# Graph layer chain on one core: in the pruning loop, the load of a later block is issued ahead of the store of the pruned block

## The chip, the cores and the metric

The kernel runs on 1 core of one Trainium2 chip. The metric is the device time of one execution in microseconds (us). A core has five engines that run their own instruction streams and meet at semaphores: TensorE (PE), VectorE (DVE), ScalarE (ACT), GpSimd (POOL) and SyncE (SP), which here issues nearly all transfers (DMAs). The page counts 16 DMA engines for them.

## The reference, cut to what matters

x is 4096 x 64, adj is a 4096 x 4096 matrix of float32 (64 MB) with about 0.2% of its entries nonzero. Four graph layers follow one another, each with a residual and a layer norm. The third (L2) runs two iterations of an attention and pruning layer with H = adj; of an iteration, this is what the change touches:

```python
# x_comp: x times the mask of nodes that stay; xn: its rows normed
cos = xn @ xn.T
edge_scores = jax.nn.softmax(cos * H / TAU, axis=1)
edge_mask = (edge_scores >= th_edge) & comp_mask[:, None]
H_pruned = H * edge_mask
connectivity = H_pruned.sum(axis=1)
...
edeg = jnp.maximum(H_pruned.sum(axis=0), EPS)
...
agg = H_pruned.T * dv_isqrt[None, :] @ transformed
msg = dv_isqrt[:, None] * (H_pruned @ agg * de_inv[:, None])
```

(The last two lines are joined here.) So each row block of H is read, scored, pruned and written to memory, and the whole of H_pruned is read again afterwards.

## The kernel before, in words

The matrix doesn't fit on the core, so each pass streams it in 32 row blocks of 128 x 4096 float32, 2 MB (2048 KB) each. The passes run in phases, one after the other, with a barrier of all engines between phases. The two iterations (`for it in range(2)`) each have an attend phase, which scores all blocks against edge features, and a prune phase. In the prune phase, after a short part that makes the mask of nodes, comes the pruning loop over n = 0 to 31, written out without a hardware loop. The block of step n is `seq[n]`.

The buffers of the loop: `held`, 5 slots (HELD = 5) for blocks of H as read, block n in slot n % 5; and `prod`, 3 slots (SL3 = 3), block n in slot n % 3, for its scores, which are turned in place into exponentials and then into the pruned block. Blocks 0 to 3 are still there from the attend phase; `load(R)` with R = 4 loads block 4 at the start.

The work of block n on the engines:

- TensorE (`score_products`, L848) makes the scores in four chunks of 1024 columns in PSUM; later (`column_sum`, L866) it adds up the columns of the pruned block. That waits for `pruned`.
- DVE (`weighted_scores`, L884) multiplies each of the four chunks with the block of H into `prod` and takes the row maximum (L889).
- ScalarE (`exponentials`, L895) takes exp in place with the row sum.
- DVE (`prune`, L1205 and L1210) compares with the threshold, multiplies with H, and writes the pruned block into `prod`, counting up `pruned`.
- SP (L1080) stores the pruned block to `Hp` ("pruned" in the profile), counting `stored`.

DVE's order is: scores of block n + 1, pruning of block n, scores of block n + 2, pruning of block n + 1, and so on. Before the scores of block n it waits for three things: that block n is loaded (`loaded[n % 5]`), that the store of block n - 3, from the same `prod` slot, has landed (`stored[n % 3]`), and that the column sums of block n - 3 are done (`summed`).

SP runs one queue of instructions in order. In step n it waits until block n is pruned, then issues two DMAs: the store of block n (L1080), and the load of block n + 5 (L1075) into the `held` slot that the pruning of block n has just set free. Steps 27 to 31 have no load. In steps 28 and 29 SP also issues the first two loads of chunks of `Hp` (`load_chunk`, L1066) for what follows, after waiting for stores of much earlier steps; the third comes once all scores are made, the rest after all stores landed. All these DMAs go to the same queue.

After the loop, the gather and scatter part reads `Hp` in 32 chunks and is mostly TensorE work.

Of the kernel before, what the change touches and what calls it, by code (L numbers as in the profile page):

```python
# [88 lines left out]
def build(nc, d):  # L89
    ctx = ExitStack()  # L90
    with ctx:
# [57 lines left out]
        Hp = nc.dram_tensor("pruned", (NB, P, N), F32, kind="Internal").ap()  # L149
# [456 lines left out]
        with phase("l0") as (block, sem):  # L606
# [24 lines left out]
            @block.sync  # L631
            def _(sp):
                for dst, src in first_loads:
                    sp.dma_start(dst, src).then_inc(first_loaded, 16)
                sp.wait_ge(twice_zero, 1)
                for dst, src in first_diagonal:
                    sp.dma_start(dst, src).then_inc(first_loaded, 16)
# [66 lines left out]
        with phase("l1") as (block, sem):  # L704
# [38 lines left out]
            def side(pe):  # L743
# [9 lines left out]
                       seq=[*range(24, NB), *range(24)], slots=range(8), resident=8, counted=range(8, NB))  # L753
# [62 lines left out]
        def half_blocks(m):  # L816

            half, k = divmod(m, HB)
            pair = adjT_b[NB - 2 - 2 * k:NB - 2 * k]
            return pair.rearrange("n p c -> p n c")[:, :, HALF * half:HALF * half + HALF]

        def two_half_blocks(s):

            return stream[:, s, :].rearrange("p (n c) -> p n c", n=2)

        SOFT = ("part_max", "all_max", "bias_ready", "part_sum", "all_sum")
        SL3 = 3  # L830
# [3 lines left out]
        prod = [stream[:, 3 + s, :] for s in range(3)]  # L834
# [63 lines left out]
        for it in range(2):  # L898
# [4 lines left out]
            with phase(f"i{it}_attend") as (block, sem):  # L903
# [6 lines left out]
                seq = [30, 31, 26, 27, 28, 29, *range(26)]  # L910
# [61 lines left out]
            with phase(f"i{it}_prune") as (block, sem):  # L972
# [52 lines left out]
                stored = [sem(f"block_stored{s}") for s in range(SL3)]  # L1025
# [5 lines left out]
                seq = [*range(22, NB), *range(22)]  # L1031
# [20 lines left out]
                def first_row(c):  # L1052
                    return (24 + 8 * c) % NB
# [7 lines left out]
                @block.sync  # L1061
                def _(sp):
                    def load_chunk(x):
                        g, c = divmod(x, CH)
                        rows_c = slice(first_row(c), first_row(c) + 8)
                        sp.dma_start(chunk_slot[x % 3].rearrange("p (n j) -> p n j", n=8),  # L1066
                                     Hp[rows_c].rearrange("n p j -> p n j")[:, :, BANK * g:BANK * g + BANK])\
                            .then_inc(chunk_loaded[x % 3], 16)

                    def wait_stored(blocks):  # L1070
                        for s in range(SL3):
                            sp.wait_ge(stored[s], 16 * len(range(s, blocks, SL3)))

                    def load(n):
                        sp.dma_start(held[n % HELD], adj_b[seq[n]]).then_inc(loaded[n % HELD], 16)  # L1075

                    load(R)
                    for n in range(NB):
                        sp.wait_ge(pruned, n + 1)
                        sp.dma_start(Hp[seq[n]], prod[n % SL3]).then_inc(stored[n % SL3], 16)  # L1080
                        if n + HELD < NB:
                            load(n + HELD)
                        if n == 28:
                            wait_stored(10)
                            load_chunk(0)
                        if n == 29:
                            wait_stored(18)
                            load_chunk(1)
                    wait_stored(26)
                    sp.wait_ge(scores_ready, NB * NC)  # L1090
                    load_chunk(2)
                    wait_stored(NB)
                    for x in range(3, groups * CH):
                        sp.wait_ge(gathered, x - 2)
                        sp.wait_ge(turned, x - 2)
                        load_chunk(x)
                    if last_it:
                        sp.wait_ge(gathered, groups * CH)
                        sp.dma_start(starts, starts_kept).then_inc(next_ahead[4], 16)
                    for done, slots_free in ((groups - 1, (2, 3)), (groups, (0, 1))):  # L1100
                        sp.wait_ge(scattered, done)
                        for s in slots_free:
                            if last_it:
                                sp.dma_start(two_half_blocks(s), half_blocks(s)).then_inc(next_ahead[s], 16)
                            else:
                                sp.dma_start(stream[:, s, :], adj_b[s]).then_inc(next_ahead[s], 16)
# [374 lines left out]
```

## Time and profile before

| what | value |
|---|---|
| median of 3 runs | 2464.47 us (2464.37 to 2468.63) |
| profiled execution | 2466.14 us, its span 2464.0 us |
| busy, share of the span | PE 84%, DVE 72%, ACT 32%, POOL 0% |
| DMA moved | 834.15 MB, mean 339 GB/s |
| granted TensorE clock over the span | 0.929 of full speed |
| first pruning loop, first store to last | 724.8 to 1033.0 us |
| second pruning loop, first store to last | 1675.5 to 1981.3 us |

Times in the profile are us from the start of the span. "Busy" counts compute instructions only; waiting and issuing DMAs are not in it. A DMA's time to landing runs from its issue to the last increment of its semaphore, so it holds the time that it queues behind earlier DMAs. An idle stretch in front of an instruction is put down to the releaser; "issue" stands where the profile shows no engine that released it.

### The profile page before, as it was taken

The numbers are of one execution on the slowest core, as the hardware profiler recorded it, in microseconds if no ns is written. First come the engines' busy times: TensorE is split into PE (matmuls) and PEld (weight loads), VectorE is DVE, ScalarE is ACT, GpSimd is POOL, SyncE is SP. The second block draws the span as 40 slices with busy tenths as digits, with TensorE's granted clock in tenths as the row PEclk, the third lists the DMA queues.
The fourth block names the chain that finished last, engine by engine and source line by source line (L and its number), as shares of the span: only waits on it lengthen the run. The fifth ranks groups of instructions, "written<-read, shape, count | busy, mean of one in ns | idle before, by whom it ended". The sixth has DMA issues, their size and how long they took to land. (4 is left out here: it accounts for less than half of the span.)

```text
span 2464.0 us, 36357 instructions
## 1 busy us (share of the span) xinstructions
PE 2065.9 (84%) x15608; PEld 737.9 (30%) x15608; DVE 1763.4 (72%) x2035; ACT 781.9 (32%) x990; POOL 4.5 (0%) x18
## 2 busy tenths in 40 slices
PE   6798959889977677699999979987676779996898
PEld 2224334223321111133334323231111134443333
DVE  7875983158879999865553228869999975554898
ACT  0001001046643333311110016654333311111897
POOL 0000000000000000000000000000000000000000
PEclk9998989999988888799999999988888889998999
DMA  9975989989939999977778989947999987773796
GB/s 384 421 325 241 428 354 382 429 326 378 378 126 422 413 413 403 374 265 258 276 265 347 427 335 381 372 185 329 422 414 410 381 329 274 274 274 155 298 420 255
DMA packets 123484, 834.15 MB, mean 339 GB/s; under 512 B 8512, under 2 KB 10560, under 8 KB 76608
## 3 DMA queue, kind: packets, MB, share of 16 engines
q1 hardware_dynamic: 121136, 829.48, 84.1%
q8 instruction: 121, 1.98, 0.3%
q10 hardware_dynamic: 2192, 2.40, 0.3%
q14 instruction: 35, 0.29, 0.0%
HBM read 695.54 MB, written 136.31 MB: 338 GB/s over the span
## 5 line engine op out<-in xcount | busy, mean ns | idle before, releaser
L895 ACT ACTIVATE stream<-stream,negmax 128x4096 f32<-128x4096 f32 x128 | 475.1, 3712 | 521.2 <-DVE negmax L889 521.2
L884 DVE CUSTOM_DVE_ANT_0 stream<-ps,stream 128x1024 f32<-128x1024 f32 x352 | 414.6, 1220 | 54.2 <-PE ps L848 32.3
L428 PE MATMUL ps<-stream,stage 128*64 128x512 f32 x1792 | 403.1, 600 | 55.5 <-DMA stream<-in_adjT 28.8
L848 PE MATMUL ps<-edgeT,node_twice 64*128 64x512 f32 x1024 | 295.2, 698 | 179.0 <-DVE mx L884 178.9
L848 PE MATMUL ps<-edgeT,query_twice 64*128 64x512 f32 x1024 | 249.6, 619 | 6.5 <-DVE edgeT L916 3.9
L1170 PE MATMUL ps<-stream,xw 32*64 32x512 f32 x4096 | 228.3, 589 | 0.8 <-ACT xw L1252 0.6
L428 PEld LDWEIGHTS ps<-stream,stage 128*64 128x64 f32 x1792 | 127.0, 138 | 324.1 <-issue 252.0
L848 PEld LDWEIGHTS ps<-edgeT,node_twice 64*128 64x128 f32 x1024 | 96.8, 207 | 363.9 <-DVE mx L884 259.9
L866 PE MATMUL ps<-stream,ones 128*1 128x512 f32 x1024 | 176.8, 826 | 9.5 <-DVE stream L1210 9.5
L1210 DVE SCALAR_TENSOR_TENSOR stream<-stream,cut 128x4096 f32<-128x4096 f32 x40 | 179.4, 4484 | 1.4
L1387 DVE SCALAR_TENSOR_TENSOR query_twice<-stream,query_twice 128x512 bf16<-128x512 f32 x256 | 154.8, 685 | 4.8 <-ACT query_twice L1365 4.7
L1365 ACT ACTIVATE query_twice<-ps,less_one_exponent 128x512 int32<-128x512 int32 x256 | 154.2, 686 | 10.5 <-PE ps L1421 8.1
L1277 DVE STREAM_TRANSPOSE stream<-spare 128x4096 f32<-128x4096 f32 x22 | 97.6, 4437 | 78.7 <-PE ps L1170 55.9
L406 ACT ACTIVATE stage<-moved 128x64 f32<-128x64 f32 (+1 forms) x128 | 29.4, 252 | 373.4 <-PE ps L428 322.5
L884 DVE CUSTOM_DVE_ANT_0 stream<-ps,spare 128x1024 f32<-128x1024 f32 x112 | 131.9, 1220 | 17.9 <-PE ps L848 9.3
L1242 ACT COPY curT<-ps 128x512 f32<-128x512 f32 x16 | 9.4, 586 | 413.0 <-PE ps L1142 413.0
L1170 PEld LDWEIGHTS ps<-stream,xw 32*64 32x64 f32 x4096 | 102.8, 132 | 123.9 <-issue 120.9
L848 PEld LDWEIGHTS ps<-edgeT,query_twice 64*128 64x128 f32 x1024 | 88.4, 187 | 169.1 <-DVE mx L884 103.5
L1277 DVE STREAM_TRANSPOSE stream<-query_twice 128x4096 f32<-128x4096 f32 x22 | 97.5, 4430 | 54.9 <-PE ps L1170 34.3
L1277 DVE STREAM_TRANSPOSE stream<-node_twice 128x4096 f32<-128x4096 f32 x20 | 88.7, 4433 | 57.4 <-PE ps L1170 37.1
L866 PE MATMUL ps<-stream,rz 128*1 128x512 f32 x1024 | 122.5, 598 | 6.1 <-DVE rz L954 6.1
L1431 PE MATMUL ps<-query_twice,stream 128*64 128x512 bf16 x768 | 106.0, 384 | 8.5 <-DVE stream L1394 7.3
(196 smaller groups left out, 1684.3 us busy)
## 6 DMA issues: line engine op xcount, KB each, us to landing
stream<-in_adj SPq DMA_DIRECT2D x140, 2048.0 KB, 13.8
stream<-in_adjT SPq DMA_DIRECT2D x74, 2048.0 KB, 12.9
pruned<-stream SPq DMA_DIRECT2D x64, 2048.0 KB, 10.6
spare<-in_adj SPq DMA_DIRECT2D x26, 2048.0 KB, 10.0
spare<-pruned SPq DMA_DIRECT2D x22, 2048.0 KB, 11.0
query_twice<-pruned SPq DMA_DIRECT2D x22, 2048.0 KB, 11.3
node_twice<-pruned SPq DMA_DIRECT2D x20, 2048.0 KB, 11.5
query_twice<-in_adj SPq DMA_DIRECT2D x12, 2048.0 KB, 15.7
```

What stands on the lines that cost most here:

```text
L406: nc.scalar.activation(stage[:, t.k % SL, :], natural_block(moved, t.block), ACT.Copy)\
L428: last = nc.tensor.matmul(ps[F * h:F * h + F, bank + b, :], stage[:, t.k % SL, :], half_bank(src, b, h), start=False, stop=False, skip_gro ...
L848: last = nc.tensor.matmul(ps[:, 2 * slot + h, :], stationary[F * h:F * h + F, rows_n], bank_of(edgeT[F * h:F * h + F, :], c), start=True, ...
L866: last = nc.tensor.matmul(ps[32 * g:32 * g + 1, 6 + half, :], w, bank_of(src, 4 * half + g), start=False, stop=False, skip_group_check=True)
L884: nc.vector.tensor_tensor_reduce(out=prod[s][:, cols], in0=ps[:, 2 * slot:2 * slot + 2, :].rearrange("p a b -> p (a b)"), in1=block_in[:, ...
L895: nc.scalar.activation(prod[s], prod[s], ACT.Exp, bias=negmax[:, s:s + 1], accum_out=zsum[:, s:s + 1]).then_inc(exp_done, 1)
L1170: last = nc.tensor.matmul(ps[F * h:F * h + F, q, :], agg[g % 2][r, b, :], src[r, :, b, :], start=g == 0 and b == 0, stop=g == groups - 1 a ...
L1210: nc.vector.scalar_tensor_tensor(out=prod[s], in0=prod[s], scalar=cut[:, s:s + 1], in1=buffer(t), op0=ALU.is_ge, op1=ALU.mult, accum_out=s ...
L1277: v.transpose(turned_pair[y % 3][:, N * (x % 2):N * (x % 2) + N], chunk_slot[x % 3])\
L1365: nc.scalar.activation(bank_of(clean, c).bitcast(I32), ps[:, c, :].bitcast(I32), ACT.Relu, bias=less_one_exponent[:, :], scale=1.0).then_i ...
L1387: v.scalar_tensor_tensor(out=bank_of(weight[u % 2], c), in0=bank_of(edges, c), scalar=0.0, in1=bank_of(clean, c), op0=ALU.not_equal, op1=A ...
L1431: last = nc.tensor.matmul(ps[F * h:F * h + F, 4 + 2 * half + q, :], natural_block(support[i], NB - 1 - k), bank_of(weight[u % 2], 2 * q + ...
```

## The change

Two statements of SP's loop trade places: within a step, the load of block n + 5 is issued first and the store of block n second. The wait for `pruned` stays ahead of both. In steps 27 to 31, which have no load, nothing differs. Instructions, bytes, buffers and semaphores are the same.

```diff
                     load(R)
                     for n in range(NB):
                         sp.wait_ge(pruned, n + 1)
-                        sp.dma_start(Hp[seq[n]], prod[n % SL3]).then_inc(stored[n % SL3], 16)
                         if n + HELD < NB:
                             load(n + HELD)
+                        sp.dma_start(Hp[seq[n]], prod[n % SL3]).then_inc(stored[n % SL3], 16)
                         if n == 28:
                             wait_stored(10)
                             load_chunk(0)
```

## Rows read from the trace of the kernel before

**Rows 1.** The page: busy time and share; DMA issues with median time to landing.

```profile
PE 2065.9 (84%) x15608; PEld 737.9 (30%) x15608; DVE 1763.4 (72%) x2035; ACT 781.9 (32%) x990; POOL 4.5 (0%) x18
...
pruned<-stream SPq DMA_DIRECT2D x64, 2048.0 KB, 10.6
```

**Rows 2.** Windows: length, busy per engine (instructions), TensorE clock, DMA share, GB/s.

```profile
724.70:1008.20 283.50, 203.39 (x896) 52.31 (x896) 263.69 (x338) 106.47 (x56) 0.00 (x0) 0.83 0.99 407
1675.40:1957.40 282.00, 199.03 (x896) 52.61 (x896) 263.69 (x337) 106.48 (x56) 0.00 (x0) 0.84 0.99 410
1033.50:1060.00 26.50, 19.44 (x80) 7.62 (x72) 19.83 (x16) 3.93 (x6) 0.73 (x2) 0.66 0.72 279
744.00:1000.00 256.00, 182.35 (x800) 46.81 (x800) 236.45 (x303) 95.07 (x50) 0.00 (x0) 0.83 1.00 413
```

**Rows 3.** Waits of DVE, first and second loop: us in total, times, longest.

```profile
DVE stream L884 <- issue: 17.1, 23, 1.7
...
DVE stream L884 <- issue: 15.1, 22, 1.4
```

**Rows 4.** Timeline of SP's queue: start us, length us, instruction.

```profile
724.82 0.33 SPq L1080 DMA_DIRECT2D pruned<-stream  x1
725.20 0.43 SPq L1075 DMA_DIRECT2D stream<-in_adj  x1
...
998.51 10.09 SPq L1080 DMA_DIRECT2D pruned<-stream  x2
1008.72 0.38 SPq L1066 DMA_DIRECT2D spare<-pruned  x1
...
1675.53 0.33 SPq L1080 DMA_DIRECT2D pruned<-stream  x1
...
1744.39 0.33 SPq L1080 DMA_DIRECT2D pruned<-stream  x1
...
1754.17 0.33 SPq L1080 DMA_DIRECT2D pruned<-stream  x1
...
1764.64 0.33 SPq L1080 DMA_DIRECT2D pruned<-stream  x1
...
1774.22 0.33 SPq L1080 DMA_DIRECT2D pruned<-stream  x1
...
1947.44 10.43 SPq L1080 DMA_DIRECT2D pruned<-stream  x2
```

**Rows 5.** Landing of DMAs issued at 724.8, 1008.7, 700.4, 1744.4, 1774.2, and 735 to 910.

```profile
pruned<-stream SPq DMA_DIRECT2D x1, 2048.0 KB, 7.2
stream<-in_adj SPq DMA_DIRECT2D x1, 2048.0 KB, 11.8
...
spare<-pruned SPq DMA_DIRECT2D x1, 2048.0 KB, 12.3
...
query_twice<-in_adj SPq DMA_DIRECT2D x1, 2048.0 KB, 7.9
...
pruned<-stream SPq DMA_DIRECT2D x1, 2048.0 KB, 10.5
...
pruned<-stream SPq DMA_DIRECT2D x1, 2048.0 KB, 10.7
...
pruned<-stream SPq DMA_DIRECT2D x17, 2048.0 KB, 10.7
stream<-in_adj SPq DMA_DIRECT2D x11, 2048.0 KB, 15.4
```

**Rows 6.** Timeline of DVE: score instructions with the idle time before them.

```profile
1744.69 1.22 DVE L884 CUSTOM_DVE_ANT_0 stream<-ps,query_twice 128x1024 f32<-128x1024 f32 x1 [0.33 <-issue]
1755.03 1.22 DVE L884 CUSTOM_DVE_ANT_0 stream<-ps,stream 128x1024 f32<-128x1024 f32 x1 [0.88 <-issue]
1785.11 1.23 DVE L884 CUSTOM_DVE_ANT_0 stream<-ps,spare 128x1024 f32<-128x1024 f32 x1 [0.31 <-issue]
1009.41 1.23 DVE L884 CUSTOM_DVE_ANT_0 stream<-ps,stream 128x1024 f32<-128x1024 f32 x1 [1.16 <-issue]
```

## The prediction

> **What bounds the kernel now.** I read the page from the top: shares of the span, the 40 slices, then the DMA issues [rows 1]. VectorE (DVE) is busy 72% of the whole span, TensorE 84%; neither says what limits the pruning loops, so I cut the two loops out by windows [rows 2]. Each window is 283.5 and 282.0 us long, runs from the first store of a pruned block to the end of step 27, and holds DVE at 263.7 us in both: 93%. The DMA engines stand at 0.99 and 407 to 410 GB/s. TensorE is at 203.4 and 199.0 us, 70%, ScalarE at 38%. So the loop has two limits close together: DVE and the transfers.
>
> The view of waits for DVE in these stretches has one entry that matters: the scoring instruction at L884 idles 17.1 us in 23 places in the first loop, 15.1 us in 22 in the second [rows 3]. The releaser is called "issue", no compute engine, which leaves the DMA waits in front of the scores. There are two: the load of block n+3 (`loaded`) and the store of block n (`stored`), since `prod` has three slots. To tell them apart I set landings beside the restarts. In the second loop the store was issued at 1744.39 and landed 10.5 us later, at 1754.9, and DVE restarted at 1755.03; the store of 1774.22 took 10.7, landed at 1784.9, and DVE restarted at 1785.11 [rows 4, 5, 6]. The restart follows a store's landing by about 0.15. Loads land after a median 15.4 us [rows 5], while block n+5, whose load is issued when block n is pruned, is first read some three intervals later, about 30 us. So in each step the transfer that DVE waits for is the store, and the load has about 14 us to spare.
>
> **How one step runs.** Let I(n) be the moment SP sees block n pruned and issues its first DMA. DVE's order is score n+2, prune n+1, score n+3, prune n+2. From the start of score n+2 to I(n+1) it takes 9.48 us (1744.69 to 1754.17) or 9.61 us (1755.03 to 1764.64) [rows 4, 6]; I take 9.55. Score n+3 starts at I(n+1) or at the landing of store n plus 0.15, whichever is later. Where the store decides, I(n+2) = I(n) + landing + 0.15 + 9.55. With a landing of 10.6 that gives 20.3 per two steps, 10.15 per step. Measured: 27 intervals in 273.7 us (724.82 to 998.51), 10.14 each, and 271.9 in the second loop, 10.07 [rows 4]. The rule reproduces the loop before. The 10.6 itself is queueing: the step moves 4.19 MB, at 413 GB/s 10.15 us [rows 2], so a store finds some 3.4 us of the previous load ahead of it (10.6 against 7.2 for a store alone).
>
> **The change, part by part.** Instruction counts, bytes and semaphores stay. In 27 steps of each loop (n from 0 to 26) load n+5 is issued before store n; steps 27 to 31 have no load and are unchanged.
>
> *The issue itself.* The store issues about 0.4 us later, the load about 0.4 earlier [rows 4]; both fit into SP's idle time, some 9 us per step. POOL issues no DMA here, and every transfer of the loop is in SP's one queue. TensorE's column sums wait on `pruned`, not on a transfer, and the chunk loads of steps 28 and 29 stay behind their stores and wait for stores long landed. The delay is inside the landing below and not added.
>
> *The earlier load: worth nothing.* DVE has no wait that ends with a load, and the slack is 14 us. Its lead removes no stall.
>
> *The later store: the term of the sum.* The trace has two DMAs issued together on a drained queue at the first step of each loop: the store lands after 7.2, the load issued 0.38 behind it after 11.8, that is 12.2 after the first issue [rows 4, 5]. The second transfer is thus served after the first, 5.0 us behind. Turned round, the store becomes the second one. How a store behind a load lands on a drained queue is not in the trace. The bounds: the 10.6 of today's backlogged store below (then no loss, or a gain of the tail's 1.2 us below), and a load alone plus a store alone above, 7.9 + 7.2 = 15.1. Nearer rows: 12.2 as above; a chunk load behind a store, 0.45 + 12.3 = 12.75; and load alone 7.9 plus one service of 5.0 = 12.9 [rows 4, 5]. I take 12.5, between the near rows.
>
> Does the queue drain? With 12.5, I(n+2) = I(n) + 12.5 + 0.15 + 9.55 = I(n) + 22.2, 11.1 us per step against 10.15 of transfer. So yes: the 3.4 us backlog, which today delays every store, is gone, and this pays for part of the load that now stands ahead. Without it the store would land 5 us later, not 1.9.
>
> *The sum.* I(28) is set by I(0) and 14 such double steps: 14 x 22.2 = 310.8 us. Before it was 1008.27 - 724.82 = 283.45 and 1957.54 - 1675.53 = 282.01 (the merged rows give the second of their two issues as start + length - 0.33) [rows 4]. That is 27.35 and 28.8 more, 56.1 together. Back comes the tail: before, score 30 waited 1.16 us at 1009.41 because store 27 still found a backlog [rows 6]; after, it finds none. I give 1.2 back for both loops. Net +54.9. Behind the loop the order is unchanged, so later phases shift.
>
> On that point the Trainium skill (DMA: Bandwidth & Descriptors, Anatomy of one DMA) fits a software-issued DMA as 2.0 us plus bytes over 436 GB/s. By it a store behind a load would land after some 11.6 us and the sum would be about +30 us, an estimate that coincides with the cheaper case below; the row of the two together, 12.2, is longer, so I keep the rows.
>
> The profiled execution took 2466.14 us, 2.14 around its span of 2464.0; the change brings it to 2521.0. The median of the runs, 2464.47, lies 1.67 below that execution, so the forecast is 2519.
>
> **The rivals.**
>
> A dearer pair. Landing at 12.9 with 9.61 for DVE gives 22.66 per double step, 317.2 in all, +33.8 and +35.2, less 1.2: +68, 2532. For it: load alone is 0.7 slower than store alone, and that may sit in front of everything behind it. If the store doesn't start moving before the load has landed (15.1), it is 24.8 x 14 = 347.2, +128, 2592; against it speaks that the second transfer follows the first by 5.0, not 7.9.
>
> A cheaper pair. If a drained queue moves the two transfers faster than a full one, the landing could come halfway between today's 10.6 and my 12.5, an estimate of 11.6. That gives 21.3 per double step, 298.2 in all, +14.8 and +16.2, less 1.2: +30, 2494. For it: in the first pair the second landing came 5.0 after the first, a little under the 5.08 that half of a 10.15 us step makes, so full speed is there from the start; against it: only the one pair shows it, and by no more than 0.1.
>
> No change: the two transfers move side by side instead of one after the other. Then the order of issue counts 0.4 us and the backlogged 10.15 per step stays: about 2464 to 2468. Against it: at the first step side-by-side transfers would land both near 12, and the first landed at 7.2. The Trainium skill (same page, Queues, rings and completion order) says that a later descriptor may finish its write before an earlier one; by that rule this rival would be live. The rows show the order kept within 2 MB transfers.
>
> Faster: the clock. TensorE's granted clock is 0.83 in both loops and 0.66 in the 26.5 us around the end of the first one, with 19.4 us of TensorE work there [rows 2]. The two levels are 1.2 and 2.4 GHz, so both mix them. If the store hid and longer pauses let the clock rise, this stretch could give up to 19.4 x 0.34 = 6.6 us, twice 13, with the tail 14: 2450. It decides only from a store landing of at most 9.4 us, where DVE never stops; against it stand all 17 landings at a median of 10.7 from step 1 on [rows 5]. Without the hiding, the same clock gain may trim a few us from the forecast.
>
> **How the numbers follow.** The forecast case (landing 12.2 to 12.8: 21.9 to 22.5 per double step, +46 to +63, that is 2510 to 2527) 0.55; dearer 0.13; cheaper 0.20; no change 0.08; faster 0.04. The range takes in the forecast case, the cheaper case down to 2494 and the dearer up to 2535. This kernel's measurement tells 0.2%, about 5 us, from no change. Faster 0.04, same 0.08, slower 0.88.
>
> **What the profile would show.** Stores issued some 0.4 us behind their loads; the first store landing about 12.1 after its own issue instead of 7.2, loads at about 8 instead of 15.4; DVE stalled in front of L884 about 1.5 us per step on average, some 40 us in each loop instead of 17, in uneven pairs (the second interval near 12.6); a mean interval of 11.1; DMA share down from 0.99 to about 0.91; DVE busy unchanged at 263.7. Wrong would be: intervals still at 10.1 with the queue full (side by side), a stall that ends with a load, or a loop as long as before with the loss elsewhere.

## The result: 5.2% slower, 2594.5 us, outside the range and past the forecast

The changed kernel takes 2594.53 us median (2589.4 to 2601.2, 4 runs) against 2466.55 us for the kernel before on the same chip; ratio 1.052, interval 1.0502 to 1.0538. That is 128 us more. I forecast 2519, range 2494 to 2535. The sign and the place were right, the size was not: the loss is 2.3 times the forecast, and equals what I worked out for a store landing of 15.1 us (2592) and put aside as a bound.

The profiled execution took 2596.86 us, its span 2594.8. The windows of the two loops after the change, to be read beside [rows 2] (columns as there):

```profile
724.90:1075.10 350.20, 223.11 (x896) 55.48 (x896) 264.54 (x339) 106.46 (x56) 0.00 (x0) 0.77 0.91 330
1738.00:2087.00 349.00, 213.60 (x896) 54.02 (x896) 266.20 (x337) 108.06 (x58) 0.00 (x0) 0.78 0.90 331
```

The same instructions, DVE's busy time the same within 2.5 us, but 350 and some 347 us instead of 283.5 and 282.0. The bytes are the same, so the rate fell from 407 to 330 GB/s. TensorE's granted clock fell as well, from 0.83 to 0.77, and its 896 instructions took 20 us more in the first loop; DVE's part of a step, from the landing of store n to I(n+2), stayed at 9.6 to 9.8 us, so that cost nothing here. From I(28) of the first loop to I(0) of the second it is 665 us after and 667 before; the whole difference lies in the two loops.

SP's queue after, to be read beside [rows 4] (start, length, instruction); the first steps, then, in one row, the store of the last pair and the two stores behind it:

```profile
725.05 0.33 SPq L1075 DMA_DIRECT2D stream<-in_adj  x1
725.43 0.43 SPq L1082 DMA_DIRECT2D pruned<-stream  x1
734.55 0.33 SPq L1075 DMA_DIRECT2D stream<-in_adj  x1
...
749.36 0.33 SPq L1075 DMA_DIRECT2D stream<-in_adj  x1
...
759.93 0.33 SPq L1075 DMA_DIRECT2D spare<-in_adj  x1
...
774.39 0.33 SPq L1075 DMA_DIRECT2D query_twice<-in_adj  x1
...
1050.69 24.77 SPq L1082 DMA_DIRECT2D pruned<-stream  x3
```

The intervals begin in uneven pairs, 9.5, 14.8, 10.6, 14.5 us, and even out towards the end (12.3 to 12.8 between 986.85 and 1036.68). From I(0) to I(28) = 1050.69 + 24.77 - 0.33 = 1075.13 it is 350.1 us, 14 double steps of 25.0. Before, it was 283.45, 20.25 each. In the second loop 1740.37 to 2087.74, 347.4 us: +66.6 and +65.4.

The landings, from the DMAs of the first step and those issued from 735 to 1050 us, beside [rows 5]:

```profile
stream<-in_adj SPq DMA_DIRECT2D x1, 2048.0 KB, 9.6
pruned<-stream SPq DMA_DIRECT2D x1, 2048.0 KB, 14.1
...
pruned<-stream SPq DMA_DIRECT2D x25, 2048.0 KB, 15.1
stream<-in_adj SPq DMA_DIRECT2D x14, 2048.0 KB, 10.4
```

With the 0.4 us that it is issued behind the load, the store lands 14.5 us after I(0) in the first step, and 14.1 to 16.2 after I(n) in the rest of the first loop. Over the even steps, which carry the chain from I(0) to I(28), the mean is 15.25 in the first loop and 15.0 in the second. By the rule of the prediction 15.25 + 0.15 + 9.55 = 24.95 per double step; 25.0 was measured. The rule held, the landing that went into it did not.

DVE's waits in the first loop and its restarts, beside [rows 3] and [rows 6]:

```profile
DVE stream L884 <- issue: 77.6, 26, 4.9
DVE stream L884 <- DMA pruned<-stream: 5.2, 1, 5.2
...
739.75 1.23 DVE L884 CUSTOM_DVE_ANT_0 stream<-ps,spare 128x1024 f32<-128x1024 f32 x1 [5.23 <-DMA pruned<-stream]
750.32 1.23 DVE L884 CUSTOM_DVE_ANT_0 stream<-ps,query_twice 128x1024 f32<-128x1024 f32 x1 [0.98 <-issue]
764.77 1.22 DVE L884 CUSTOM_DVE_ANT_0 stream<-ps,stream 128x1024 f32<-128x1024 f32 x1 [4.87 <-issue]
```

82.8 us idle instead of 17.1, a difference of 65.7 for a loop that grew by 66.6. This time one row names the store. No row names a load, and each load lands some two steps before its block is read.

### The profile page after: what moved, and what is told of

It is laid out like the page before. It is cut to its first block and busy times, and to the rows that moved or that the text cites. A ratio compares the mean times of both kernels' runs of the same rounds, so it can differ in the third digit from the quotient of the medians.

```text
span 2594.8 us, 36357 instructions
## 1 busy us (share of the span) xinstructions
PE 2100.2 (81%) x15608; PEld 749.2 (29%) x15608; DVE 1764.7 (68%) x2035; ACT 781.6 (30%) x990; POOL 6.6 (0%) x18
## 5 line engine op out<-in xcount | busy, mean ns | idle before, releaser
L848 PE MATMUL ps<-edgeT,node_twice 64*128 64x512 f32 x1024 | 306.6, 721 | 276.4 <-DVE mx L884 276.3
L884 DVE CUSTOM_DVE_ANT_0 stream<-ps,stream 128x1024 f32<-128x1024 f32 x352 | 415.2, 1220 | 124.7 <-issue 91.4
L866 PE MATMUL ps<-stream,ones 128*1 128x512 f32 x1024 | 198.4, 917 | 9.5 <-DVE stream L1210 9.5
L884 DVE CUSTOM_DVE_ANT_0 stream<-ps,spare 128x1024 f32<-128x1024 f32 x112 | 132.2, 1220 | 45.8 <-issue 25.1
L1365 ACT ACTIVATE query_twice<-ps,less_one_exponent 128x512 int32<-128x512 int32 x256 | 154.2, 685 | 10.1 <-PE ps L1421 7.7
L1170 PEld LDWEIGHTS ps<-stream,xw 32*64 32x64 f32 x4096 | 108.4, 132 | 117.6 <-issue 111.7
## 6 DMA issues: line engine op xcount, KB each, us to landing
stream<-in_adj SPq DMA_DIRECT2D x140, 2048.0 KB, 10.4
stream<-in_adjT SPq DMA_DIRECT2D x74, 2048.0 KB, 13.1
pruned<-stream SPq DMA_DIRECT2D x64, 2048.0 KB, 14.8
```

The source lines that it names most:

```text
L848: last = nc.tensor.matmul(ps[:, 2 * slot + h, :], stationary[F * h:F * h + F, rows_n], bank_of(edgeT[F * h:F * h + F, :], c), start=True, ...
L866: last = nc.tensor.matmul(ps[32 * g:32 * g + 1, 6 + half, :], w, bank_of(src, 4 * half + g), start=False, stop=False, skip_group_check=True)
L884: nc.vector.tensor_tensor_reduce(out=prod[s][:, cols], in0=ps[:, 2 * slot:2 * slot + 2, :].rearrange("p a b -> p (a b)"), in1=block_in[:, ...
L1170: last = nc.tensor.matmul(ps[F * h:F * h + F, q, :], agg[g % 2][r, b, :], src[r, :, b, :], start=g == 0 and b == 0, stop=g == groups - 1 a ...
L1365: nc.scalar.activation(bank_of(clean, c).bitcast(I32), ps[:, c, :].bitcast(I32), ACT.Relu, bias=less_one_exponent[:, :], scale=1.0).then_i ...
```

## The experiments

The question that the result left: why does a store behind a load land after 15, where the trace of before had a load behind a store at 12.2? Nine kernels ran. Three of them hold nothing but transfers.

**Pairs by themselves.** VectorE only paces SP here; blocks of zeros are stored, blocks of adj are loaded.

```diff
+for _ in range(6): store(); load(); drain()      # S,L on a drained queue
+for _ in range(6): load(); store(); drain()      # L,S on a drained queue
+...                                              # a load, the store 2.2 or 4.5 us behind it
+...                                              # ten pairs at 10.4, 10.9, 12.2 us, in both orders
```

> A kernel of transfers alone, none of the layers is computed: 2 MB loads and stores of 128 x 4096 blocks on SP's queue, one by one, in pairs on a drained queue, a load with a store 2.1 or 4.6 us behind it, and pairs paced by VectorE at about 10.3, 11.1 and 12.5 us in both orders. Known from the two traces: load alone lands after 7.9, store alone 7.2, store then load 12.2, load then store 14.5 with the load itself at 9.6. Theory A, the neighbour: a load is slowed while its first reads are under way and a store's descriptors stand right behind it. It expects load then store at 14 to 15 here too with the load at 9.5 or more, and with the store 4.6 us behind the load lands at 7.9 to 8.1. Theory B, the order: a store behind a load is late by itself (load 7.9, store 14 to 15) at any distance. Theory C, the compute engines of the real loop slow it: load then store at 12.2 to 12.8 here. Paced at 10.3, A and B expect store first at 7.5 to 11 and load first at 14 to 16, C the two within 1 us of 12.5.

Measured, median times to landing of each issue. In this order: four loads alone, four stores alone, six pairs S,L, six pairs L,S, three loads with the store 4.5 us behind; then the pairs paced at 10.37 us, store first and load first:

```profile
dst<-in_adj SPq DMA_DIRECT2D x4, 2048.0 KB, 7.7
...
pruned<-src SPq DMA_DIRECT2D x4, 2048.0 KB, 6.3
...
pruned<-src SPq DMA_DIRECT2D x6, 2048.0 KB, 7.2
dst<-in_adj SPq DMA_DIRECT2D x6, 2048.0 KB, 11.8
...
dst<-in_adj SPq DMA_DIRECT2D x6, 2048.0 KB, 8.6
pruned<-src SPq DMA_DIRECT2D x6, 2048.0 KB, 13.1
...
dst<-in_adj SPq DMA_DIRECT2D x3, 2048.0 KB, 7.6
pruned<-src SPq DMA_DIRECT2D x3, 2048.0 KB, 8.0
...
pruned<-src SPq DMA_DIRECT2D x10, 2048.0 KB, 7.2
dst<-in_adj SPq DMA_DIRECT2D x9, 2048.0 KB, 11.8
...
dst<-in_adj SPq DMA_DIRECT2D x9, 2048.0 KB, 10.9
pruned<-src SPq DMA_DIRECT2D x9, 2048.0 KB, 15.4
```

S,L takes 11.8 + 0.4 = 12.2, to the tenth the real kernel's first step before. L,S takes 13.1 + 0.4 = 13.5. The load of such a pair lands 0.9 later than alone, and so it does with the store 2.2 us behind (8.4 to 8.8); with the store 4.5 us behind it is back at 7.6 to 8.0. A store with a load behind it is late by the same 0.9: 7.2 against 6.3 alone, so the 7.2 that the prediction calls a store alone was not one. The same kernel also issued pairs of one kind: there the first is not delayed (load 7.6, store 6.3) and the second lands at 12.5 and 11.2. So it is a transfer of the other kind behind it that delays the first (one kernel, four to six pairs of each sort). That is what theory A said, at half its size: it expected 14 to 15. Theory B is out (the load is slowed by the store next to it), and so is C for these 13.5 us (no compute is needed); the changed kernel's first pair, at 14.5, is 1.0 above the median and 0.3 above the longest of the six here.

The paced rows matter more. Store first at 10.37 us per pair, each pair lands at 7.2 and 12.2 as on a drained queue. Load first at the same pace has its first store at 13.4, the second already at 15.3 and the last at 16.0. Most of that rise is one step of 1.9 us behind the first pair: from the second store to the last it is 10.45 us per pair (854.2 to 937.8, eight intervals), little more than the pace. And a slower pace doesn't cure it. At 11.25 us per pair, in the same kernel, the pairs behind the first:

```profile
dst<-in_adj SPq DMA_DIRECT2D x9, 2048.0 KB, 10.3
pruned<-src SPq DMA_DIRECT2D x9, 2048.0 KB, 14.8
```

That is 14.7 to 15.9 us after the pair's first issue, mean 15.3, without growing, where store first at 11.25 stays at 7.2 and 12.2. At 12.6 us load first is back at a median of 13.5. What differs between the three paces is how far the pair before still is from landing when a pair is issued: about 5, 4 and 0.9 us. That this is the reason is likely from these rows, not shown.

**The lead and the depth.** The same kind of kernel; first a pair with more behind it, then ten paced pairs with four transfers ahead of them in the queue.

```diff
+begin(); issue("SLSL")
+for _ in range(10): wait for the tick (10.37 us); issue(order)      # "SL", then "LS"
```

> Transfers alone again, nothing of the layers is computed. A first 2 MB transfer, and 0.4, about 2.2 or about 4.6 us behind it a second kind: S then L; S then L,S; L then S; L then S,L, four times each; then pairs paced at 10.36 us on a queue that got four transfers ahead, in both orders. Theory of the lead: a load that has waited behind enough work in the queue is served in 4.9 us, one that was issued when little was left takes longer. It expects the load to land 4.9 after the store ahead of it at lead 0.4, and 5.5 to 7.5 after it at lead 4.6 with a second store right behind the load. Paced with four ahead, both orders should keep their pace with landings that don't grow, where load first grew from 13.4 to 16 us on the drained queue. Theory of the order: load first loses at any depth and its landings grow by 0.5 or more per pair here too.

Measured: on a drained queue S then L has the load at 12.2; with one more store issued 0.5 us behind the load, it lands at 13.3 to 13.9. With a lead of 4.5 us it is 13.1 to 13.6. That is 6.6 to 7.0 behind the store ahead, as the theory of the lead expected, but at lead 0.4 it is 6.1 to 6.7 too, where that theory expected 4.9. The lead changed little, and the theory is wrong in that form: what costs is the store behind the load. The paced pairs with four ahead, eight of store first and nine of load first:

```profile
pruned<-src SPq DMA_DIRECT2D x8, 2048.0 KB, 15.4
dst<-in_adj SPq DMA_DIRECT2D x8, 2048.0 KB, 20.3
...
dst<-in_adj SPq DMA_DIRECT2D x9, 2048.0 KB, 16.0
pruned<-src SPq DMA_DIRECT2D x9, 2048.0 KB, 20.5
```

Both orders shrink their landings (load first from 22.9 to 19.7 us after the pair's issue), 10.0 us per pair. In a deep queue the order costs nothing. The theory of the order falls.

**The uneven pace, quiet and with compute beside.** Pairs at 10.8 and 13.8 us by turns, close to the changed kernel's before its intervals even out.

```diff
+for k in range(82): ScalarE copies 128x4096 float32        # in the third and fourth stretch
+for k in range(500): TensorE multiplies 128x128 by 128x512 # there too
```

> Transfers alone, nothing of the layers computed, in pairs at the uneven pace of the changed kernel (about 10.7 and 14.2 us by turns): store first quiet, load first quiet, load first with ScalarE copying 128x4096 blocks and TensorE multiplying all the time, store first with the two beside. In the changed kernel the store of a load-first pair lands 15.0 to 16.0 after the pair's first issue, in the kernel of transfers at an even 12.2 us pace 13.1 to 13.5 after it. Theory of the queue: the uneven pace alone explains it, the quiet load-first pairs land at 14.5 to 16 behind a short interval and near 14 behind a long one. Theory of the neighbours in SBUF: quiet pairs stay at 13.5 and those with compute beside land 1 us or more later. Store first should stay at 7.2 and 12.2 in either case after a long interval.

Measured: store first stays at 7.2 and 12.2, quiet or not, but for two of the 24 pairs (13.1 and 13.6). Load first, the last eleven of each stretch, quiet, then with compute beside:

```profile
dst<-in_adj SPq DMA_DIRECT2D x11, 2048.0 KB, 9.8
pruned<-src SPq DMA_DIRECT2D x11, 2048.0 KB, 14.4
...
dst<-in_adj SPq DMA_DIRECT2D x11, 2048.0 KB, 10.0
pruned<-src SPq DMA_DIRECT2D x11, 2048.0 KB, 14.8
```

Quiet pairs behind a short interval land 15.1 to 15.7 after their first issue, those behind a long one 13.4 to 14.8. Their mean is 14.6, with compute beside 15.0, in the changed kernel 15.2. So the pace gives most of the landing by itself; compute beside adds 0.4, no more than single pairs scatter. It is not the unevenness as such: the even 11.25 us above gave 15.3. Where the pair before had at most 1.5 us to go, the kernel's stores landed at 13.7 to 15.3 (mean 14.7), the quiet ones behind a long interval at 13.9 in the mean: that much, some 0.8 us, is the kernel's own.

**Half the swaps.** Load first in even steps only, 14 of the 27 pairs.

```diff
+if n % 2 == 0 and n + HELD < NB: load(n + HELD)
 sp.dma_start(Hp[seq[n]], prod[n % SL3]).then_inc(stored[n % SL3], 16)
-if n + HELD < NB:
+if n % 2 and n + HELD < NB:
     load(n + HELD)
```

> The load goes ahead of the store in steps with even n alone, 14 of the 27 pairs of each loop. Theory of the chain: I(n+2) = I(n) + landing of store n + 0.15 + 9.55, so the swapped even steps alone set the pace; with their stores landing 13.5 to 15.4 after the step's first issue a double step is 23.2 to 25.1 us and the total 2545 to 2595, more than half of the loss with half of the swaps. Theory of the queue (each swapped pair costs its 2.4 us of transfer time): half of the 128 us, 2520 to 2535.

Measured 2574.33 and 2585.17 us (ratio 1.0461, 1.0435 to 1.0487): +114 us, 89% of the loss with half of the swaps; the chain's 2545 to 2595 holds it, the queue's 2520 to 2535 does not. SP's queue and the landings of the step at 771.36 (load, store) and of the next store, issued at 780.73; the last queue row holds two loads, the second at 781.40 + 14.38 - 0.33 = 795.45:

```profile
746.79 0.33 SPq L1075 DMA_DIRECT2D stream<-in_adj  x1
...
771.36 0.33 SPq L1075 DMA_DIRECT2D query_twice<-in_adj  x1
...
781.40 14.38 SPq L1075 DMA_DIRECT2D stream<-in_adj  x2
...
query_twice<-in_adj SPq DMA_DIRECT2D x1, 2048.0 KB, 9.4
pruned<-stream SPq DMA_DIRECT2D x1, 2048.0 KB, 13.9
...
pruned<-stream SPq DMA_DIRECT2D x1, 2048.0 KB, 9.8
```

The double step from 771.36 to 795.45 is 24.1 us, and 13.9 + 0.4 + 0.15 + 9.55 = 24.0; the mean of the 14 double steps is 24.2. The unswapped store lands at 9.8, early, and that helps nobody: the chain of even steps sets the pace. This is the chain rule, shown by an experiment that a cost per swapped pair would have put at +64.

**The wait moved one block on.** A fourth slot for pruned blocks (`query_twice`, taken from the blocks read), so that the scores of block n+4, not n+3, wait for store n; in both orders. The first chunk loads behind the loop come in another order.

```diff
+prod4 = [*prod, q2[:, :]]
-HELD = 5
+HELD = 4
-sp.dma_start(Hp[seq[n]], prod[n % SL3]).then_inc(stored[n % SL3], 16)
+sp.dma_start(Hp[seq[n]], prod4[n % 4]).then_inc(stored[n % 4], 16)
```

> The kernel before with four slots for the pruned blocks and four for the blocks read, so that the scores of block n+4 wait for the store of block n; 28 loads in the loop, and the first chunk loads after it come some 10 us later than before. No wait of VectorE should end with a store: interval 10.1 to 10.2, set by the transfers (4.19 MB at 413 GB/s), or less if the stalls fed back. Total 2465 to 2495, more than before for the later chunks alone.

> The same four slots with the load issued ahead of the store. If the loss of the change goes through VectorE's wait for the store alone, the interval is 10.1 to 10.4 and the total within 10 us of the store-first twin. If the order itself lowers the rate of the queue (16 DMA engines at 0.91 share but 330 GB/s in the changed kernel), the interval stays at 11 or more and the total is 50 us or more above the twin.

Measured: store first 2452.53 us (ratio 0.9944, 0.9921 to 0.9966), load first 2451.65 us (0.9949, 0.9926 to 0.9971). The two orders can't be told apart, and both beat the kernel before. The loop of the first, and the landings from 850 to 1000 us of store first, then load first:

```profile
724.00:1008.00 284.00, 207.17 (x945) 53.96 (x948) 275.69 (x359) 110.36 (x59) 0.00 (x0) 0.85 1.01 426
...
pruned<-stream SPq DMA_DIRECT2D x11, 2048.0 KB, 14.6
...
pruned<-stream SPq DMA_DIRECT2D x11, 2048.0 KB, 19.2
```

A landing of 19.2 us, 4 more than what cost 128 us, costs nothing with the fourth slot. I expected 10.1 to 10.4 per step, set by transfers; it was 9.49 (732.43 to 1017.10, 30 intervals), DVE at 97% and the queue at 426 GB/s. DVE's waits in the first loop, store first, then load first (L885 is the L884 of before):

```profile
DVE stream L885 <- DMA stream<-in_adj: 4.2, 11, 1.7
DVE query_twice L885 <- DMA spare<-in_adj: 1.3, 5, 0.3
...
DVE stream L885 <- issue: 4.3, 11, 1.7
DVE query_twice L885 <- issue: 1.7, 5, 0.6
```

So DVE still waits a little, 5.5 and 6.0 us, for the second landing of a pair (load first, a store issued at 876.97 lands at 896.17 and DVE restarts at 896.28): with about four transfers in the queue it moves 430 GB/s (850 to 1000 us), a pair takes some 9.7 us in either order, and the loop has DVE and the transfers as limits side by side. The fourth slot does two things at once. It gives the store one more step before anyone waits, and it lets the queue grow deep, where the order costs nothing (the paced pairs above). The runs show that the two together remove the loss, not which share each has.

**Load ahead, but not side by side.** Load n+4 issued when DVE begins to prune block n, 4.6 us ahead of store n; three slots.

```diff
+if n >= 1 and n + HELD - 1 < NB:
+    sp.wait_ge(max_ready, n + 2)
+    load(n + HELD - 1)
 sp.wait_ge(pruned, n + 1)
 sp.dma_start(Hp[seq[n]], prod[n % SL3]).then_inc(stored[n % SL3], 16)
-if n + HELD < NB:
-    load(n + HELD)
```

> The kernel before with each load issued half a step ahead of the store, when VectorE begins to prune (load n+4 about 4.6 us ahead of store n), so that the queue holds load, store, load, store as after the change, with the two not side by side. Theory A (neighbour) expects 10.1 to 10.3 per step and 2460 to 2475 in all. Theory B (any load ahead of a store) expects 11.5 or more per step and 2550 or more.

Measured 2491.14 and 2502.07 us (ratio 1.0121, 1.0067 to 1.0175), between the two expectations: +30 us. The landings from 760 to 910 us:

```profile
pruned<-stream SPq DMA_DIRECT2D x14, 2048.0 KB, 11.9
stream<-in_adj SPq DMA_DIRECT2D x8, 2048.0 KB, 11.6
```

The store lands 1.2 later than before, by the chain rule 0.6 us per step, 34 us over 56 steps. So this load ahead in the queue costs about a quarter of the loss. That doesn't show what standing side by side costs: the load took 11.6 here, no less than in the changed kernel, and the store landed 4.9 us behind it in both. The store gained because its load had been issued 4.6 us earlier.

**Two queues.** The load on SP's queue, the store on ScalarE's, both at the pruning.

```diff
+exponentials(act, last_step(n, seq), max_ready, exp_done)
+if n >= 1: store(act, n - 1)        # waits for pruned, then issues on ScalarE's queue
```

> The load is issued by SP when block n is pruned, and the store by ScalarE at the same moment, on ScalarE's own DMA queue. If a store is late because it stands behind the load in one queue, two queues let the two share the engines: the store lands 10 to 13 after the pruning, interval 10.2 to 11.3, total 2465 to 2530. If the mix of a load and a store side by side is what costs, in one queue or two, the store lands at 14 or later and the total is 2560 or more.

Measured 2551.43 and 2558.39 us (ratio 1.036, 1.034 to 1.0381), just short of the second case. Landings from 735 to 910 us:

```profile
pruned<-stream ACTq DMA_DIRECT2D x15, 2048.0 KB, 14.9
stream<-in_adj SPq DMA_DIRECT2D x9, 2048.0 KB, 14.2
```

Here load and store do move side by side, and end side by side: 12.6 and 12.8 in the first pair, on a drained queue, and 12.5 to 15.2 for the 27 stores, mean 14.0. For the one that is waited for this is little better than standing behind the other: 89 of the 128 us stay.

**Four slots, chunk buffers changed.** Store first; chunks 0 and 1 go to buffers that come free at the last pruned blocks.

```diff
+prod4 = [q2[:, :], *prod]
-chunk_slot = [spare_block, slot[6], slot[7]]
+chunk_slot = [slot[7], slot[6], spare_block]
```

> The four-slot kernel, store first, with the chunk loads behind the loop given other buffers (node_twice first, then query_twice, spare last), so that the second and the third chunk are issued at the last pruned blocks and not after the last store. The twin with four slots was at 2452.5. The chunks start 5 to 8 us earlier per loop, which TensorE may use only where it waited for them: 2438 to 2452. If the transfers at the end of the loop are the limit (queue backlog of 19 us), no gain over the twin.

Measured 2447.15 us (2442.52 to 2450.66, 4 runs; ratio 0.9917, 0.9901 to 0.9934), the fastest kernel here. Its interval overlaps with the twin's, so the gain of the buffers alone is not shown; that of the fourth slot is.

## Why the prediction was wrong

**The bound, DVE's wait for the store, and no wait for a load: right.** The idle time in front of L884 grew by 65.7 us in the first loop, the loop by 66.6. Nothing was gained from the earlier load.

**The rule of the double step: right.** I(n+2) = I(n) + landing + 0.15 + 9.55 gives 24.95 against 25.0, and 24.0 against 24.1 in the kernel with half the swaps, where it put the effect of the untouched odd steps at nothing.

**The landing of the store behind a load: the term that failed.** I took 12.5 us; in the steps of the chain it was 15.25 in the mean of the first loop and 15.0 in the second. 14 x 2.75 + 14 x 2.5 = 74 us of store landing too little, of the 76 by which the loops outgrew the forecast (+132.0 measured, +56.1 forecast). I had read 12.2 from a load behind a store and taken the order as nearly indifferent, since "The second transfer is thus served after the first, 5.0 us behind". That half holds: after the change the store lands 4.9 us behind its load in most pairs. What I missed is in front: the load itself. Alone it lands at 7.9, with a store next to it at 9.6 in the first step and 10.4 to 10.9 in the loop. The kernels of transfers allow an estimate of how the 2.7 us divide: 1.0 is the pair on a drained queue (13.5), 1.1 more comes with a pair before it that has not landed (mean 14.6 at the uneven pace), and the remaining 0.6 belongs to the whole kernel, of which compute beside may be 0.4.

**The queue drains, and that pays for part of the load: wrong.** The DMA share fell to 0.91, but the queue was not empty when the next pair came: in both loops each pair was issued 0.2 to 5.5 us before the store of the pair before had landed. For store-first pairs at 10.37 us the 1.8 us left did no harm (7.2 and 12.2), for load-first pairs what is left counts (13.5 with 0.9 us left, 15.3 with 4). I had the DMA share at about 0.91 as a sign that I was right; it came out at 0.91, for another reason: 330 GB/s at 0.91 is a slower engine, not an idler one.

**10.15 us of transfer per step: right for that depth of queue, wrong as a limit of the engines.** In the kernel before the first stores land at 7.2, 8.0, 9.7 and 10.8 us, so there the queue did fill at steps of 9.5 us. With four slots it moved 426 to 430 GB/s and the step was 9.49 us.

**The rivals.** "Dearer pair" had the right sign, and its far end, 15.1 us and 2592 us, met the result by luck. It added 7.9 for a load alone and 7.2 for a store alone; the 7.2 is a store with a load behind it. The kernel of transfers has 7.7 and 6.3 alone, 14.0 together, and the result lies above that. Nor does the store wait for the load to land as that end supposed: it lands 4.9 behind it, not 6.3 or 7.2. I argued against that end with the 5.0 us between two landings, a row that measures what the second transfer adds and says nothing of what it does to the first. "No change" (side by side) is out for one queue. "Faster" is out: TensorE's granted clock fell. The rule of the Trainium skill (DMA: Bandwidth & Descriptors, Queues, rings and completion order) that a later descriptor may finish its write before an earlier one is not tested by these rows. A landing is the last increment of a semaphore, and by the same section an increment lands only after every earlier write of its DMA engine. What the rows show is that in one queue the second of a pair always landed last, some 5 us behind the first. Its fit (same page, Anatomy of one DMA), made for software-issued transfers, gave 11.6 us for the store behind a load; 13.5 was measured without compute, so the measurement decides.

**What stays open.** Why a store behind a load slows the load, and why a load ahead of a store costs only while the queue is shallow. No run looked inside the DMA engines, and the 0.6 to 0.8 us between the quiet uneven pairs and the kernel were not followed further. All pairs were 2 MB blocks between the same two tensors; whether other sizes or places in memory behave alike was not tried.

## What to carry to other kernels

Before moving a DMA in a queue, ask which landing an engine waits for, and put that one first; if what it waits for must come second, give it another slot, which here made the order worthless and the kernel 0.5 to 0.8% faster than before. Where a chain runs over every second step, half of a bad change costs nearly all of it. A landing read for one order of transfers is not the landing for the other: measure the pair by itself, in both orders and at the pace of the loop. Adding up the two transfers alone is no upper bound: 7.7 + 6.3 = 14.0 here, and the store behind a load landed at 15.2 in the mean.

## What the runs showed of the hardware that I had not expected

- 2 MB blocks of 128 x 4096 float32 on a drained queue: load alone 7.7 us, store alone 6.3; store then load 7.2 and 12.2; load then store 8.6 and 13.5. The first is delayed by 0.9 when a transfer of the other kind stands behind it, and not at all by one of its own kind (load 7.6, store 6.3).
- Ten store-first pairs at 10.37 us each landed at 7.2 and 12.2. Load first, the stores behind the first landed at 15.0 to 16.4 at that pace, at 14.7 to 15.9 at 11.25 us, and at a median of 13.5 at 12.6. With four transfers ahead, both orders took 10.0 us per pair.
- In the changed kernel the DMA engines show a share of 0.91 while they move 330 GB/s, before 0.99 and 407. A high share does not say that the engines move what they can.
- A load and a store on two queues, issued together, landed at 12.6 and 12.8 us on drained queues, and at 14.2 and 14.9 in the median from 735 to 910 us.
